# One-hot rows of the expert picks on VectorE, and a three-subtraction split on GpSimd, in an attention and mixture-of-experts kernel

## The chip, the cores and the metric

The kernel runs on one core of a Trainium2 chip. The metric is the device time of one execution in microseconds (us). The engines are named as in the profile: PE is TensorE, DVE is VectorE, ACT is ScalarE, POOL is GpSimd, and SP (SPq its queue) issues most transfers. TENSOR_TENSOR is an elementwise operation with two tensor inputs, TENSOR_SCALAR one with a tensor and constants, CAST a copy that changes the type.

## The reference

Input x is 8 sequences of 512 rows of 128 numbers. The first layer is a linear attention with Fourier features, 16 heads of 8:

```python
q = x @ Wq.T + bq; k = x @ Wk.T + bk; v = x @ Wv.T + bv          # split into 16 heads of 8
feat(z) = concat(cos(z @ proj / sqrt(8)), sin(z @ proj / sqrt(8))) / sqrt(128)
kv  = sum over the rows l of feat(k)[l] (outer) v[l]              # per sequence and head
x   = layernorm(x + (feat(q) @ kv) @ Wo.T + bo)
```

The second layer routes each row to 2 of 8 experts (128 to 512 to 128, with relu):

```python
route = softmax(x @ Wr + br); keep the two largest, divide by their sum
x = layernorm(x + sum over the 2 picks of route[e] * (relu(x @ W1[e] + b1[e]) @ W2[e] + b2[e]))
```

Everything is float32 in and out.

## The kernel before

The program is written out by hand: each engine has its own list of instructions, in order, and semaphores tie the lists together. No planner is at work; the number u at which a piece stands in an engine's loop is the order.

**Attention stage.** Eight bodies, one for each sequence b, 16 units u each. Units 0 to 7 are keys, units 8 to 15 queries; a unit is 128 x 1024 angles. For each unit PE multiplies into the PSUM tensor `ang` (L570, L574), DVE rounds to whole turns (`round_turns`, L1067), PE subtracts the turns (L583), ACT takes two sines (L873, L874), and the second is squared (`square`), on POOL for u in (1, 3, 4, 6, 8, 10, 12) (L1430) and on DVE for the others (L1075). PE then uses the features in `kv_product` (L603, keys) and `out_product` (L638, queries). In body b the loops of DVE and POOL square unit u - 2 at step u.

**Pieces of other sequences in body b.** ACT evacuates k and q of sequence b + 1 (L859 a bf16 part, L861 the float32 value `qk_f`), and POOL splits each into three bf16 parts (`split`, L354, L356, L358, at u = 7 and u = 9), which SP writes to DRAM and reads back stacked. For sequence b - 1 comes the end of the first layer and the routing: `residual`, `statistics`, `moments` (DVE), `rsqrt` (POOL), `normalize` (ACT), logits (PE, L665), `take_logits` and `largest` (DVE, u = 10), `which` (DVE, u = 10, after the square of that step: the indices of the picks, `idx8`, as u32). At u = 11 POOL runs `chosen`: it makes two one-hot rows of 8 from each row's picks (`hot`), adds them (`picks`, L1542), and writes three numbers beside the row that will be sent. PE counts ranks from `picks` (`ranks`, L675 to L680, at u = 12), DVE adds the base (`slot_m`, L1141, u = 12), POOL multiplies by `hot` (L1553, u = 13), DVE reduces to slot numbers, and POOL sends the rows to their expert's region with eight indirect transfers (L1561, u = 14 and 15). PE's list at u = 12 is: the angles, L583 of the unit before, `kv_turn` (L614 to L617), `ranks`; then u = 13 with L574, L583 and `out_product` (L638), which waits for the DVE evacuation `kv_evac` (L1086, L1087), which stands behind `round_turns` of unit 12. DVE's list at u = 11 is `round_turns`, `kvT_evac` (L1079), `square` of unit 9.

In body 7 there is no split. POOL builds the table of expert tiles for the first six sequences in its place (`early_counts` to `early_table`, L1454 to L1502), and `chosen(6)` stands behind it.

**Expert stage.** 71 tiles of 128 rows. SP loads a tile, PE turns it and runs the two layers (L775, L786, L795), DVE evacuates (L1306, L1314, L1354), ACT copies the weights and scales, POOL adds a bias for some tiles (L1572) and sends the results (L1591). The routing of sequence 7 is interleaved: `which` at DVE's tile step 18, `chosen` at POOL's step 20, `ranks` at PE's step 22. Last, the two picks of each row are summed and normalized.

A `hold` in the code is a wait. `over` broadcasts a tensor; `idx8` is 128 x 4 x 8 u32, `iota` the numbers 0 to 7.

Of the kernel before, what the change touches and what calls it, by code (L numbers as in the profile page):

```python
# [23 lines left out]
ALU = mybir.AluOpType  # L24
# [67 lines left out]
def build(nc, x, proj, Wq, bq, Wk, bk, Wv, bv, Wo, bo, W1, b1, W2, b2, Wr, br,  # L92
# [8 lines left out]
    with ctx:  # L101
        def sb(name, shape, dt=F32):
            return ctx.enter_context(nc.sbuf_tensor(name, shape, dt))
# [38 lines left out]
        lg = sb("lg", [P, LT, EXP])  # L142
        top8 = sb("top8", [P, LT, EXP])
        idx8 = sb("idx8", [P, LT, EXP], U32)
        pick_no = sb("pick_no", [P, LT, TOPK])
        hot = sb("hot", [P, TOPK, LT, EXP])
        picks = sb("picks", [P, LT * EXP], F16)
        slot_m = sb("slot_m", [P, LT, EXP])
# [60 lines left out]
        def cut(n):  # L209
# [38 lines left out]

            "y_ok", "bo_ok", "ln_stat", "ln_aggr", "ln_eps", "ln_pow", "ln_shift", "xn_ok", "xr_mm", "xr_ev",

            "lg_mm", "lg_ok", "top_ok", "idx_ok", "no_ok", "off_ok", "hot_ok", "picked", "meta", "rk_mm", "slot_ok", "based",
            "slotk_ok", "slots_ok", "scattered", "pads_at", "pads_in", "rt", "tab_ok",

            "et", "et_half", "w1_in", "w2_in", "b1_in", "b2_in", "b1_mm", "b1_ok", "bp_mm", "bp_ev", "b2_mm", "b2_ok", "gap_ok", "gate_ok", "xbg_ok",
# [64 lines left out]
        def over(v, shape):  # L319

            return v.broadcast_to(shape)
# [21 lines left out]
        def sequences(body):  # L343

            for b in range(BATCH):
                body(b, b % RING)

        def split(eng, b, side):

            wait(eng, "kq"[side] + "_ev", 1, b, 1)  # L350
            f = qk_f[:, side, :]
            p = parts[:, side, :, :]
            n = 3 * side
            eng.tensor_tensor(f, f, p[:, 0, :], ALU.subtract).then_inc(s["split"], 1)  # L354
            hold(eng, "split", 6, b, n + 1)
            eng.tensor_copy(p[:, 1, :], f).then_inc(s["split"], 1)  # L356
            wait(eng, "split", 6, b, n + 2)
            eng.tensor_tensor(p[:, 2, :], f, p[:, 1, :], ALU.subtract).then_inc(s["split"], 1)  # L358
# [634 lines left out]
        def _(dve):  # L993
# [135 lines left out]
            def which(b):  # L1129
# [2 lines left out]
                    ins = dve.max_index(idx8[:, t, :], top8[:, t, :], lg[:, t, :])  # L1132
                ins.then_inc(s["idx_ok"], 1)

            n_picks = LT * EXP

            def take_ranks(b):
# [109 lines left out]
            LAST_ROUND = ((7, bias_add), (8, bias_add))  # L1247

            BEFORE_ROUND = ((6, moments), (10, take_logits), (13, move_base))
            AFTER_ROUND = ((5, residual), (10, largest))  # L1250
            AFTER_SQUARE = ((5, statistics), (10, which), (12, take_ranks), (13, slot_numbers))

            def body(b, ph):
                first = isinstance(b, int) and b == 0
                last = isinstance(b, int) and b == BATCH - 1
                for u in range(UNITS):
# [33 lines left out]
                    if u == 15 and not last:  # L1290
# [4 lines left out]
            square(e, -2)  # L1295
            square(e, -1)

            LAST_PIECES = ((1, residual), (2, statistics), (3, moments), (16, take_logits), (17, largest), (18, which),
                           (23, take_ranks), (24, move_base), (26, slot_numbers))
            LATE_TABLE = ((27, late_counts), (29, late_ends), (31, late_starts), (32, late_table))  # L1300

# [119 lines left out]
        def _(pool):  # L1421
# [84 lines left out]
            def body(b, ph):  # L1506
                first = isinstance(b, int) and b == 0
                last = isinstance(b, int) and b == BATCH - 1
                for u in range(UNITS):
                    if not (first and u < 2):  # L1510
                        square(b, u - 2)
                    if u == 6 and not first:
                        rsqrt(1, b - 1, 0)
                    for step, piece in (EARLY_TABLE if last else ()):
                        if u == step:
                            piece()
                    if u in (7, 9) and not last:
                        split(pool, b + 1, (u - 7) // 2)
                    if first and u >= 11:
                        add_bo(pool, u - 9)  # L1520
                    if b == 1 and u == 0:
                        add_bo(pool, BATCH - 1)
                    if u == 11 and not first:
                        chosen(b - 1)
                    if u == 13 and not first:
                        slots_of_picks(b - 1)
                    if u in (14, 15) and not first:
                        send_rows(b - 1, u - 14)

            def chosen(b):  # L1530

                hold(pool, "idx_ok", 1, b, 1)
                pool.tensor_copy(pick_no[:, :, :], idx8[:, :, 0:TOPK]).then_inc(s["no_ok"], 1)
                wait(pool, "no_ok", 1, b, 1)
                for k in range(TOPK):
                    ins = pool.tensor_tensor(hot[:, k, :, :], over(iota[:, :].unsqueeze(1), tile8),
                                             over(pick_no[:, :, k:k + 1], tile8), ALU.subtract)
                ins.then_inc(s["off_ok"], 1)
                hold(pool, "off_ok", 1, b, 1)
                pool.tensor_scalar(hot[:, :, :, :], hot[:, :, :, :], 0.0, None, ALU.is_equal).then_inc(s["hot_ok"], 1)  # L1540
                wait(pool, "hot_ok", 1, b, 1)
                pool.tensor_tensor(picks[:, :], hot[:, 0, :, :].rearrange("p t e -> p (t e)"),  # L1542
                                   hot[:, 1, :, :].rearrange("p t e -> p (t e)"), ALU.add).then_inc(s["picked"], 1)
                pool.tensor_tensor(rows_s[:, :, P + 2:XW], top8[:, :, 0:1], top8[:, :, 1:2], ALU.subtract)
                pool.tensor_copy(rows_s[:, :, P:P + 1], pick_no[:, :, 0:1])
                pool.tensor_scalar(rows_s[:, :, P + 1:P + 2], rows_s[:, :, P + 1:P + 2], float(LEN), None, ALU.add)\
                    .then_inc(s["meta"], 1)

            def slots_of_picks(b):

# [98 lines left out]
```

## Time and profile before

| | |
|---|---|
| median of 3 runs | 553.1 us (549.98 to 554.34) |
| profiled execution, its own time | 551.36 us |
| its span in the trace | 549.6 us |
| granted clock of TensorE, mean | 0.959 of full |
| PE busy | 483.9 us, 88% |
| DVE busy | 427.8 us, 78% |
| POOL busy | 410.7 us, 75% |
| ACT busy | 381.0 us, 69% |

Busy times are shares of the whole span, over stages with different limits. Busy time of POOL and DVE contains time in which an instruction has begun and stands still. The attention stage fills the span up to about 360 us, the expert stage follows to about 522 us, and the sums and the last normalization close it.

### The profile page before, as it was taken

The numbers are of one execution on the slowest core, as the hardware profiler recorded it, in microseconds if no ns is written. First come the engines' busy times: TensorE is split into PE (matmuls) and PEld (weight loads), VectorE is DVE, ScalarE is ACT, GpSimd is POOL, SyncE is SP. The second block draws the span as 40 slices with busy tenths as digits, with TensorE's granted clock in tenths as the row PEclk, the third lists the DMA queues.
The fourth block names the chain that finished last, engine by engine and source line by source line (L and its number), as shares of the span: only waits on it lengthen the run. The fifth ranks groups of instructions, "written<-read, shape, count | busy, mean of one in ns | idle before, by whom it ended". The sixth has DMA issues, their size and how long they took to land.

```text
span 549.6 us, 13153 instructions
## 1 busy us (share of the span) xinstructions
PE 483.9 (88%) x4205; PEld 297.4 (54%) x4205; DVE 427.8 (78%) x907; ACT 381.0 (69%) x533; POOL 410.7 (75%) x474
## 2 busy tenths in 40 slices
PE   6698889999999999999999989689999679999914
PEld 3333344444444444444344444158999678999802
DVE  6769978988988988988988888568677475777654
ACT  2686669789789789789789689376555244565325
POOL 2279549879879889879879889857677656777645
PEclk9899989999999999999999999799999789999957
DMA  4675504705704705604605400032222123222174
GB/s 96 169 228 160 127 1 138 195 16 144 203 20 126 206 17 144 190 16 141 153 15 136 126 17 1 8 84 58 69 65 71 59 75 94 70 65 70 39 273 191
DMA packets 44447, 56.03 MB, mean 102 GB/s; under 512 B 8779, under 2 KB 31541, under 8 KB 44381
## 3 DMA queue, kind: packets, MB, share of 16 engines
q1 hardware_dynamic: 39493, 45.86, 30.5%
q0 software_dynamic: 4320, 8.95, 5.0%
q8 instruction: 36, 0.59, 0.5%
q10 hardware_dynamic: 568, 0.38, 0.2%
q14 instruction: 30, 0.25, 0.2%
HBM read 37.22 MB, written 17.94 MB: 100 GB/s over the span
## 4 chain that ended last, share of the span: by engine, by line
PE 55%; POOL 12%; DVE 12%; issue 9%; ACT 6%; DMA 2%; another core or an unknown queue 2%; SPq 1%; DVEq 0%; ACTq 0%; POOLq 0%
PE ang L786 11%; PE ang L795 10%; PE misc L603 7%; PE ang L583 5%; PE misc L638 5%; DVE turns L1067 5%; DVE feats L1075 4%; POOL feats L1430 3%; PE ang L574 3%; PE ang L570 3%; POOL routed_dram L1561 2%; PE misc L512 2%; PE misc L649 2%; ACT rows_s L893 2%
## 5 line engine op out<-in xcount | busy, mean ns | idle before, releaser
L1067 DVE TENSOR_SCALAR turns<-ang 128x1024 f16<-128x1024 f32 x128 | 155.4, 1217 | 46.4 <-PE ang L574 23.4
L873 ACT ACTIVATE feats<-ang 128x1024 f32<-128x1024 f32 x128 | 131.7, 1029 | 63.6 <-PE ang L583 61.1
L1430 POOL TENSOR_TENSOR feats<-feats 128x1024 f32<-128x1024 f32 x56 | 107.0, 1910 | 48.8 <-ACT feats L874 48.4
L874 ACT ACTIVATE feats<-ang 128x1024 f32<-128x1024 f32 x128 | 131.5, 1028 | 0.0
L1075 DVE TENSOR_TENSOR feats<-feats 128x1024 f32<-128x1024 f32 x72 | 102.5, 1423 | 0.7 <-ACT feats L874 0.6
L1591 POOL DMA_INDIRECT expert_dram<-feats x71 | 69.7, 981 | 36.3 <-DVE feats L1354 28.5
L1561 POOL DMA_INDIRECT routed_dram<-rows_s,slots x64 | 76.3, 1193 | 20.7 <-issue 18.3
L583 PE MATMUL ang<-turns,negi 128*128 128x512 f16 x256 | 77.9, 386 | 12.4 <-DVE turns L1067 10.5
L795 PE MATMUL ang<-experts,feats 128*128 x568 | 77.6, 281 | 5.5 <-DVE feats L1314 5.4
L786 PE MATMUL ang<-feats 128*128 128x128 f32 x568 | 78.1, 282 | 4.5 <-DVE feats L1306 2.2
L944 ACT ACTIVATE feats<-experts 128x644 f32 x71 | 52.5, 739 | 36.8 <-DVE feats L1354 25.3
L786 PEld LDWEIGHTS ang<-feats 128*128 128x128 f32 x568 | 70.6, 195 | 8.4 <-issue 5.2
L795 PEld LDWEIGHTS ang<-experts,feats 128*128 128x128 f32 x568 | 70.8, 196 | 6.8 <-issue 6.8
L603 PE MATMUL misc<-feats,v_pad 128*32 128x256 f32 x1024 | 70.7, 396 | 0.0
L1314 DVE TENSOR_TENSOR feats<-ang,feats 128x512 f32<-128x512 f32 x71 | 49.0, 690 | 26.5 <-PE ang L786 13.8
L638 PE MATMUL misc<-feats,kv_pad 128*32 128x512 f32 x512 | 67.8, 617 | 0.6
L570 PEld LDWEIGHTS ang<-proj_stk,stk 72*128 72x128 bf16 x512 | 30.9, 98 | 34.4 <-issue 32.6
L603 PEld LDWEIGHTS misc<-feats,v_pad 128*32 128x32 f32 x1024 | 27.3, 111 | 40.3 <-issue 29.2
L961 ACT ACTIVATE feats<-feats 128x128 f32<-128x128 f32 x71 | 28.1, 395 | 27.6 <-DVE feats L1363 20.4
L570 PE MATMUL ang<-proj_stk,stk 72*128 72x128 bf16 x512 | 39.9, 221 | 2.0 <-ACT stk L912 1.4
L583 PEld LDWEIGHTS ang<-turns,negi 128*128 128x128 f16 x256 | 21.7, 99 | 32.9 <-DVE turns L1067 15.6
L574 PE MATMUL ang<-stk,proj_stk 72*128 72x512 bf16 x128 | 39.1, 388 | 0.0
(195 smaller groups left out, 597.2 us busy)
## 6 DMA issues: line engine op xcount, KB each, us to landing
stk<-parts_dram SPq DMA_DIRECT2D x189, 96.0 KB
parts_dram<-parts SPq DMA_DIRECT2D x16, 384.0 KB, 3.6
feats<-routed_dram SPq DMA_DIRECT2D x72, 65.5 KB
feats<-expert_dram SPq DMA_DIRECT2D x16, 256.0 KB, 5.4
x_all<-attn_x SPq DMA_DIRECT2D x8, 256.0 KB, 4.8
experts<-ffn_W SPq DMA_DIRECT2D x8, 256.0 KB
out<-feats SPq DMA_DIRECT2D x8, 256.0 KB, 2.2
x_in<-attn_x SPq DMA_DIRECT2D x7, 256.0 KB
```

The costliest lines, as they stand in the source:

```text
L570: mm = pe.matmul(a[:, at:at + FEAT], stk[:, 0, hg, g, tok:tok + P], proj_stk[:, :], start=(g == 0), stop=False, skip_group_check=True)
L583: mm = pe.matmul(ang[:, slot(ph, u), t * 512:(t + 1) * 512], negi[:, :], turns[:, u % 2, t * 512:(t + 1) * 512], start=False, stop=True, s ...
L603: mm = pe.matmul(misc[32 * g:32 * g + 32, 0, 0:2 * FEAT].rearrange("p (a m) -> p a m", a=2), v_pad[:, 2 * half + t, g, hg * PADH:(hg + 1) ...
L638: mm = pe.matmul(misc[32 * g:32 * g + 32, 1, :], kv_pad[:, a, g, hg * PADH:(hg + 1) * PADH], feats[:, 2 * hg + g // 2, a, (g % 2) * LEN:(g ...
L786: mm = pe.matmul(h_bank[r % 2][:, j * P:(j + 1) * P], w_now[:, r % W_RING, j * P:(j + 1) * P], xgT[:, r % 2, :], start=True, stop=True)
L795: mm = pe.matmul(y_bank[r % 2][:, 0:P], hidT[:, r % 2, j * P:(j + 1) * P], expert(x_e)[:, j * P:(j + 1) * P], start=(j == 0), stop=(j == H ...
L873: act.activation(f[:, 0, :], a, ACT.Sin, scale=TWO_PI)
L874: act.activation(f[:, 1, :], a, ACT.Sin, scale=TWO_PI / 2).then_inc(s["sines"], 1)
L1067: dve.tensor_scalar(turns[:, u % 2, :], ang[:, slot(ph, u), :], MAGIC, -MAGIC, ALU.add, ALU.add)\
L1075: dve.tensor_tensor(f, f, f, ALU.mult).then_inc(s["sq_v"], 1)
L1430: pool.tensor_tensor(f, f, f, ALU.mult).then_inc(s["sq_p"], 1)
L1561: pool.indirect_dma_start(routed_dram, bass.IndirectOffsetOnAxis(slots[:, k, t:t + 1], 0), rows_s[:, t, :], None).then_inc(s["scattered"], 16)
```

## The change

DVE gets a piece `one_hot` that compares `iota` with the u32 indices directly, in two TENSOR_TENSORs, at u = 11 between `kvT_evac` and the square (in the expert stage at tile step 19). POOL's `chosen` loses the CAST of the indices, the two subtractions and the comparison with zero; it writes the three numbers beside the row first, waits for `hot_ok`, and then adds the one-hot rows. The split of k and q on POOL becomes three subtractions: the second part is written by a subtraction with bf16 output, the remainder by the same subtraction in float32, the third part as before. DVE's own split of sequence 0 stays.

```diff
-        pick_no = sb("pick_no", [P, LT, TOPK])
+        def split_apart(eng, b, side):
+            wait(eng, "kq"[side] + "_ev", 1, b, 1)
+            f = qk_f[:, side, :]
+            p = parts[:, side, :, :]
+            n = 3 * side
+            eng.tensor_tensor(p[:, 1, :], f, p[:, 0, :], ALU.subtract).then_inc(s["split"], 1)
+            wait(eng, "split", 6, b, n + 1)
+            eng.tensor_tensor(f, f, p[:, 0, :], ALU.subtract).then_inc(s["split"], 1)
+            wait(eng, "split", 6, b, n + 2)
+            eng.tensor_tensor(p[:, 2, :], f, p[:, 1, :], ALU.subtract).then_inc(s["split"], 1)
...
+            def one_hot(b):
+                hold(dve, "idx_ok", 1, b, 1)
+                for k in range(TOPK):
+                    ins = dve.tensor_tensor(hot[:, k, :, :], over(iota[:, :].unsqueeze(1), tile8),
+                                            over(idx8[:, :, k:k + 1], tile8), ALU.is_equal)
+                ins.then_inc(s["hot_ok"], 1)
...
-            AFTER_ROUND = ((5, residual), (10, largest))
+            AFTER_ROUND = ((5, residual), (10, largest), (11, one_hot))
...
-            LAST_PIECES = (... (18, which),
+            LAST_PIECES = (... (18, which), (19, one_hot),
...
                     if u in (7, 9) and not last:
-                        split(pool, b + 1, (u - 7) // 2)
+                        split_apart(pool, b + 1, (u - 7) // 2)
...
             def chosen(b):
                 hold(pool, "idx_ok", 1, b, 1)
-                pool.tensor_copy(pick_no[:, :, :], idx8[:, :, 0:TOPK]).then_inc(s["no_ok"], 1)
-                wait(pool, "no_ok", 1, b, 1)
-                for k in range(TOPK):
-                    ins = pool.tensor_tensor(hot[:, k, :, :], over(iota[:, :].unsqueeze(1), tile8),
-                                             over(pick_no[:, :, k:k + 1], tile8), ALU.subtract)
-                ins.then_inc(s["off_ok"], 1)
-                hold(pool, "off_ok", 1, b, 1)
-                pool.tensor_scalar(hot[:, :, :, :], hot[:, :, :, :], 0.0, None, ALU.is_equal).then_inc(s["hot_ok"], 1)
+                pool.tensor_tensor(rows_s[:, :, P + 2:XW], top8[:, :, 0:1], top8[:, :, 1:2], ALU.subtract)
+                pool.tensor_copy(rows_s[:, :, P:P + 1], idx8[:, :, 0:1])
+                pool.tensor_scalar(rows_s[:, :, P + 1:P + 2], rows_s[:, :, P + 1:P + 2], float(LEN), None, ALU.add)\
+                    .then_inc(s["meta"], 1)
                 wait(pool, "hot_ok", 1, b, 1)
                 pool.tensor_tensor(picks[:, :], ...
```

The last three instructions of `chosen` before are the same three that now stand at its head, with `pick_no` in the place of `idx8`.

## Rows read from the trace of the kernel before

**Rows 1.** Busy time by stretch: stretch, length, busy of each engine, PE clock, DMA share, GB/s
```profile
172.00:213.00 41.00, 39.30 (x363) 18.38 (x362) 35.77 (x57) 35.58 (x42) 35.80 (x36) 1.00 0.41 116
```

**Rows 2.** Chain of waits, body 4, 185 to 232 us: start, us, what
```profile
218.36 0.14 PE misc L675
...
219.12 0.43 PE ang L583 x2
...
219.66 1.92 PE misc L638 x16
```

**Rows 3.** Timeline of POOL, body 4: start, us, line, operation [idle before]
```profile
204.33 1.16 POOL L354 TENSOR_TENSOR qk_f<-qk_f,parts 128x512 f32<-128x512 f32 x1
205.56 1.48 POOL L356 CAST parts<-qk_f 128x512 bf16<-128x512 f32 x1
207.12 1.15 POOL L358 TENSOR_TENSOR parts<-qk_f,parts 128x512 bf16<-128x512 f32 x1
...
210.09 1.16 POOL L354 TENSOR_TENSOR qk_f<-qk_f,parts 128x512 f32<-128x512 f32 x1
211.31 1.49 POOL L356 CAST parts<-qk_f 128x512 bf16<-128x512 f32 x1
...
215.84 0.19 POOL L1533 CAST pick_no<-idx 128x8 f32<-128x8 uint32 x1
...
216.64 1.29 POOL L1540 TENSOR_SCALAR hot<-hot 128x64 f32<-128x64 f32 x1
218.01 0.25 POOL L1542 TENSOR_TENSOR picks<-hot 128x32 f16<-128x32 f32 x1
```

**Rows 4.** Timeline of DVE, body 4
```profile
204.39 2.18 DVE L1075 TENSOR_TENSOR feats<-feats 128x1024 f32<-128x1024 f32 x1
...
210.95 1.38 DVE L1075 TENSOR_TENSOR feats<-feats 128x1024 f32<-128x1024 f32 x1
...
216.46 1.22 DVE L1075 TENSOR_TENSOR feats<-feats 128x1024 f32<-128x1024 f32 x1
217.59 1.22 DVE L1067 TENSOR_SCALAR turns<-ang 128x1024 f16<-128x1024 f32 x1
...
219.02 0.41 DVE L1087 COPY kv_pad<-misc 128x256 f32<-128x256 f32 x1
```

**Rows 5.** One line's instructions on POOL: count, shortest/median/longest ns, first and last start
```profile
L356 POOL CAST parts<-qk_f x14: 609/1484/1491, 35.9 to 294.4; 128x512 bf16<-128x512 f32 x14
```

**Rows 6.** Timeline of POOL, body 0
```profile
40.39 2.14 POOL L354 TENSOR_TENSOR qk_f<-qk_f,parts 128x512 f32<-128x512 f32 x1
42.59 0.61 POOL L356 CAST parts<-qk_f 128x512 bf16<-128x512 f32 x1
```

**Rows 7.** Timeline of DVE, body 0
```profile
39.78 1.73 DVE L1075 TENSOR_TENSOR feats<-feats 128x1024 f32<-128x1024 f32 x1
```

**Rows 8.** Groups of DVE by line: count, busy us, mean ns, idle before
```profile
L1141 DVE TENSOR_TENSOR slot_m<-misc,base 128x32 f32<-128x32 f32 x8 | 1.5, 182 | 3.2 <-PE misc L680 3.2
```

**Rows 9.** Timeline of POOL, body 7
```profile
324.08 1.89 POOL L1430 TENSOR_TENSOR feats<-feats 128x1024 f32<-128x1024 f32 x1 [1.62 <-ACT feats L874]
...
346.35 0.19 POOL L1533 CAST pick_no<-idx 128x8 f32<-128x8 uint32 x1
...
347.15 0.38 POOL L1540 TENSOR_SCALAR hot<-hot 128x64 f32<-128x64 f32 x1
347.62 0.25 POOL L1542 TENSOR_TENSOR picks<-hot 128x32 f16<-128x32 f32 x1
```

**Rows 10.** Timeline of PE, body 7
```profile
347.93 0.21 PE L675 MATMUL misc<-picks,tri 128*128 128x32 f16 x1 [4.52 <-POOL picks L1542]
```

**Rows 11.** Busy time by stretch, body 7 behind that wait
```profile
349.00:353.00 4.00, 4.00 (x19) 0.71 (x17) 2.71 (x5) 1.94 (x2) 3.60 (x4) 0.50 0.00 0
```

**Rows 12.** Timeline of DVE, expert stage: the COPY of tile step 19
```profile
408.29 0.28 DVE L1306 COPY feats<-ang 128x128 f32<-128x128 f32 x1
```

**Rows 13.** Timeline of POOL, expert stage: the first transfer behind `chosen(7)`
```profile
408.62 1.09 POOL L1591 DMA_INDIRECT expert_dram<-feats  x1 [0.16 <-issue]
```

More of the change, by code:

```diff
@@ L249, in build @@
             "y_ok", "bo_ok", "ln_stat", "ln_aggr", "ln_eps", "ln_pow", "ln_shift", "xn_ok", "xr_mm", "xr_ev",
-            "lg_mm", "lg_ok", "top_ok", "idx_ok", "no_ok", "off_ok", "hot_ok", "picked", "meta", "rk_mm", "slot_ok", "based",
+            "lg_mm", "lg_ok", "top_ok", "idx_ok", "hot_ok", "picked", "meta", "rk_mm", "slot_ok", "based",
             "slotk_ok", "slots_ok", "scattered", "pads_at", "pads_in", "rt", "tab_ok",
@@ L1296, in _ @@
             square(e, -1)
-            LAST_PIECES = ((1, residual), (2, statistics), (3, moments), (16, take_logits), (17, largest), (18, which),
+            LAST_PIECES = ((1, residual), (2, statistics), (3, moments), (16, take_logits), (17, largest), (18, which), (19, one_hot),
                            (23, take_ranks), (24, move_base), (26, slot_numbers))
@@ L1543, in chosen @@
                                    hot[:, 1, :, :].rearrange("p t e -> p (t e)"), ALU.add).then_inc(s["picked"], 1)
[L1544 to L1547, printed above, removed]
             def slots_of_picks(b):
```

## The prediction, before the changed kernel was run

> **What bounds the kernel now.** I read the busy time by stretch first, to see whether an engine is full where the change acts. In one body of the attention stage PE works 39.30 of 41.00 us at full clock, DVE, ACT and POOL about 35.7 each [rows 1]. The chain of waits inside such a body then says who sets the end: around unit 12 it runs from one PE instruction into the next, the rank count at 218.36, the turns at 219.12, the query product at 219.66, with DVE just keeping up [rows 2]. Bodies 1 to 6 repeat this pattern; body 4 stands for the six. The timelines of POOL and DVE, laid side by side, show how close the other engines are. The sum of the one-hot rows, `picks`, is done at 218.26, a tenth before PE wants it [rows 3, 2]. `kv_pad` is done at 219.43, and PE starts on it at 219.66, a tenth after it was free at 219.55 (219.12 + 0.43) [rows 4, 2]. `round_turns` of unit 12 is done at 218.81, and PE uses it at 219.12 [rows 4, 2]. So POOL and DVE have almost no slack exactly at unit 12.
>
> Only in body 7 does a long wait stand: PE idles 4.52 us for `picks`, until 347.93 [rows 10], behind POOL's tile table. POOL itself had idled 1.62 us for ACT at 324.08 [rows 9], so what makes POOL faster ahead of 324 us can't shorten that wait beyond what ACT allows.
>
> **POOL and DVE block one another.** This decides the costs. A DVE square takes 1.22 us when nothing is in its way (216.46) [rows 4]. The one at 204.39 took 2.18 and ended at 206.57; POOL's subtraction beside it ended at 205.49, 1.08 earlier [rows 4, 3]. The one at 210.95 ended at 212.33; the subtraction beside it at 211.25, again 1.08 earlier [rows 4, 3]. The CASTs behind these subtractions end at 207.04 and 212.80, each 0.47 behind the square [rows 3, 4]. A CAST takes 0.61 when free [rows 6] and 1.48 here, and the median of 14 is 1.484 with the longest 1.491 [rows 5]: a constant, since POOL holds off the square and the square then holds off the CAST. A POOL subtraction behind a square does the same: 2.14 at 40.39, end 42.53, the square beside it ended at 41.51 (39.78 + 1.73), 1.02 earlier [rows 6, 7]. The Trainium skill has this as a rule ("SBUF — State Buffer", Who interferes with whom): GpSimd and a VectorE instruction with two SBUF inputs want the same port pair, which is locked for a whole instruction, and the one that comes second stands still. The trace agrees, in these three ends. By that rule `one_hot`, with two SBUF inputs, joins the contenders, which speaks against this change.
>
> **The split.** By the durations as they stand, three subtractions at 1.16 in the place of 1.16 + 1.48 + 1.15 save 0.32 us [rows 3], 0.64 for the two of a body. I don't take this. Free, the middle step goes from 0.61 to 1.16 [rows 6, 3], and it will meet the same square, so it costs 0.55 more: the subtraction ends at the square's end + 1.02, where the CAST ended at + 0.47. The first split ends 0.55 later. The work behind it moves with it, the second first subtraction ends at 211.80, the square of 210.95 at 212.88, and the second split ends 1.10 late. What hides it: POOL's lateness is no one's wait until step 11, and SP has most of a body to move the parts. If that cover is gone, it is 1.1 us a body. The Trainium skill puts GpSimd's two-input operations at a floor of about 2.5 cycles an element and calls one-input ones roughly line-rate ("GPSIMD Engine Reference", Elementwise — side-by-side cycle accounting, and Engine selection). By it a subtraction costs more than the CAST that it replaces, though the page of the profile shows 1.48 against 1.16; the free CAST of 0.61 agrees.
>
> **`chosen`, bodies 1 to 6.** Gone: everything from 215.84 to 218.01, 2.17 us [rows 3]. Of the comparison's 1.29 us only 0.38 is its own (347.15, DVE idle) [rows 9]; the rest is the square of 216.46, and whoever stands there next inherits it. So 1.27 is really gone, and POOL is 1.10 late by the split. Both about cancel. POOL's square ahead of `chosen` now ends near 217.0 instead of 215.9.
>
> **`one_hot` on DVE.** The nearest row is `slot_m`, of the same shape, 182 ns [rows 8]; two in a pipeline cost some 0.2 us if free. They would start at 216.46, where the square starts now [rows 4], and POOL's late square holds the port until 217.0. So they pass at 217.0 to 217.2, and DVE's square starts at 217.2 instead of 216.46. Behind it stand `round_turns` of unit 12, `slot_m` and `kv_evac`, all 0.7 late; PE has 0.1 of slack, so it takes 0.6 to 0.7. POOL's four short operations (about 0.2 each) stand partly behind that square, so `picks` is done at 218.65 to 219.1 instead of 218.26, and the ranks are 0.4 to 0.8 late on PE. These overlap and are not added. Bounds: 0.2 us a body if nothing blocks, 1.1 if POOL's short operations get the port ahead of `one_hot` and DVE's square starts at 217.6. I take 0.7, for it follows from the ends above; nothing later in the body gives it back, as the rest waits for PE. Six bodies: +4.2 (1.2 to 6.6).
>
> **Body 7.** No split here. From the start of `chosen(6)`, 346.35, to the end of `picks`, 347.87, are 1.52 us [rows 9]. New: four short operations at about 0.2, some 0.75; `hot` is long there. The wait of 4.52 [rows 10] shrinks by 0.8, and PE is late next by what is left, 3.7. PE's clock then still falls to its lower level, 0.50 [rows 11]; were it not to, the 4 us of that stretch would be 2.0 shorter. -0.8 (to -2.8).
>
> **The rest.** Body 0 has two splits and no `chosen`; squares there move both ways by about half a microsecond. I take 0, keep 0.5 each way. In the expert stage `one_hot` stands at DVE's step 19, ahead of the COPY at 408.29 [rows 12]; POOL, waiting for it, would send its next transfer at about 408.9 instead of 408.62 [rows 13], 0.3 later, and PE reads `picks` two tiles on. 0, at most 0.3.
>
> **Sum.** +4.2 - 0.8 = +3.4 us, against the profiled execution's 551.36: 554.8. Its span is 549.6, with 1.8 around it. The median of the three runs, 553.1, is 1.7 higher; all four average 552.2. From that, 555.6; I say 555.5.
>
> **Rivals.**
> *The change is hidden.* The port counts for little: `one_hot` costs its 0.2 six times, body 7 gives 0.8: +0.4, 552.5. For it: POOL is on no wait of PE in bodies 1 to 6. Against it: the constant ends.
> *A gain.* As above, and the clock holds in body 7: +1.2 - 2.8 = -1.6, about 550.5. For: it needs only a shorter wait. Against: 3.7 us of idling remain. A gain of over 1% (5.5 us) would need the whole wait gone, for which POOL would have to leave ACT behind at 324 us.
> *Slower than a measurement can hide.* At 215.84 the first of POOL's short operations starts with no pause behind the square. If POOL so keeps the port, its three ready ones (0.6) pass first, `one_hot` gets through at 217.6 to 217.8, and DVE's square at 217.8 is 1.3 late; PE then loses 1.3 a body: +7.8 - 0.8 = +7.0, 559.2. It decides from 1.05 us a body on. The Trainium skill says issue order decides who blocks ("SBUF — State Buffer", Who interferes with whom); no row here shows the order for this pair.
> *It doesn't do what it says.* The split drops a CAST but adds a subtraction: on POOL it saves nothing. That is part of the forecast.
>
> **Chances.** Over 1% is what a measurement of this kernel can tell from no change. Forecast 0.58, of it 0.12 with over 1.05 us a body net; hidden 0.20; gain 0.10, of it 0.04 over 1%; the slower rival 0.12. So faster 0.04, same 0.72, slower 0.24. Range: from the gain with its offset, 550, to the slower rival, 559.5. The forecast's own is 552 to 559.
>
> **What would show it.** Right: the middle step of the split at about 2.0 us in 13 of 14, not 1.16; the square of unit 9 starting 0.7 later after step 11 and lasting about 1.2, or starting on time and lasting longer; PE waiting for DVE ahead of L638 or for `picks` at L675 in bodies 1 to 6; these bodies 41.7 us long instead of 41.0; the wait for `picks` in body 7 at 3.7. Wrong: a middle step at 1.16 with the square at 1.22 beside it; bodies of 41.0; or a POOL that the split makes so late that PE waits for one of its squares.

## The result: 5.7% slower, where 0.6% was forecast

The changed kernel takes 583.62 us (median of 4 runs, 579.69 to 587.75), the kernel before 552.23 beside it (549.98 to 554.34). The ratio is 1.057, interval [1.048, 1.066]. I had forecast 555.5 and a range of 550 to 559.5. The profiled execution took 584.74 us, its span is 582.9 where it was 549.6, and the mean granted clock fell from 0.959 to 0.930.

The parts that I had costed came out near their forecast. First POOL in body 3 of the changed kernel (start, us, operation, idle before): the split and the sum of the one-hot rows.

```profile
177.13 1.16 POOL L353 TENSOR_TENSOR parts<-qk_f,parts 128x512 bf16<-128x512 f32 x1
178.37 2.03 POOL L355 TENSOR_TENSOR qk_f<-qk_f,parts 128x512 f32<-128x512 f32 x1
180.48 1.16 POOL L357 TENSOR_TENSOR parts<-qk_f,parts 128x512 bf16<-128x512 f32 x1
...
190.05 1.20 POOL L1554 TENSOR_SCALAR rows_s<-rows_s 128x4 f32<-128x4 f32 x1
191.23 0.24 POOL L1557 TENSOR_TENSOR picks<-hot 128x32 f16<-128x32 f32 x1
```

The middle step takes 2.03 us where the CAST took 1.48 [rows 3, 5]; the square beside it (177.19, 2.18 us, below) ends at 179.37, the step 1.03 later. DVE in the same body:

```profile
177.19 2.18 DVE L1086 TENSOR_TENSOR feats<-feats 128x1024 f32<-128x1024 f32 x1
...
189.27 0.72 DVE L1150 TENSOR_TENSOR hot<-iota,idx 128x32 f32<-128x32 f32 x2
189.91 1.24 DVE L1086 TENSOR_TENSOR feats<-feats 128x1024 f32<-128x1024 f32 x1
```

The two comparisons take 0.72, some 0.5 more than the 0.2 I took as free, and push the square behind them; in [rows 4] nothing stands ahead of that square. PE then waits 0.36 us for `picks` ahead of the ranks, and in body 7 still 3.98 where it was 4.52 [rows 10] (3.7 was forecast):

```profile
191.53 0.19 PE L686 MATMUL misc<-picks,tri 128*128 128x32 f16 x1 [0.36 <-POOL picks L1557]
...
385.19 0.21 PE L686 MATMUL misc<-picks,tri 128*128 128x32 f16 x1 [3.98 <-POOL picks L1557]
```

What I had not looked for is in the waits of the whole kernel (engine, tile and line, what it waited for: us in total, times, longest):

```profile
DVE turns L1078 <- remote: 21.1, 5, 4.8
PE ang L594 <- DVE turns L1078: 20.1, 13, 3.9
ACT feats L884 <- remote: 18.1, 4, 4.6
```

The view writes "remote", and the chain "another core", where it finds no releaser; this program has one core. The chain of the body has it as one piece:

```profile
154.74 1.21 DVE feats L1086
155.95 4.74 another core or an unknown queue
160.70 0.02 issue
160.72 1.23 DVE turns L1078
162.00 1.04 PE ang L594 x2
```

Beside it stand PE's and DVE's timelines:

```profile
154.09 0.62 PE L581 MATMUL ang<-proj_stk,stk 72*128 72x128 bf16 x8
...
157.84 0.23 PE L581 MATMUL ang<-proj_stk,stk 72*128 72x128 bf16 x1 [0.43 <-issue]
162.00 1.04 PE L594 MATMUL ang<-turns,negi 128*128 128x512 f16 x2 [3.92 <-DVE turns L1078]
```

```profile
154.74 1.21 DVE L1086 TENSOR_TENSOR feats<-feats 128x1024 f32<-128x1024 f32 x1
160.72 1.22 DVE L1078 TENSOR_SCALAR turns<-ang 128x1024 f16<-128x1024 f32 x1 [4.77 <-remote]
```

`round_turns` at 160.72 needs the angles that PE is recorded as making from 154.09 to 154.71, and DVE was free at 155.95. ACT and SyncE go on at 160.76 and 160.81 too. Everything that waits for PE stands still at once and goes on at once. Such a stall stands at the head of each of the bodies 2 to 7, 3.4 to 5.1 us long (by what DVE waits); none stands in body 1, for POOL sends nothing at the end of body 0. The one of body 7 looks different: there PE's own matmuls (L707, L581) are recorded in small groups from 342.63 to 348.55, with 0.2 to 1.0 us of idle time between them, and DVE waits 5.07 us for them by name. What it does to a body is read by stretch (stretch, length, busy time of PE, PEld, DVE, ACT, POOL, clock, DMA share, GB/s), against [rows 1]:

```profile
149.00:197.00 48.00, 41.78 (x366) 18.85 (x362) 36.83 (x59) 35.66 (x44) 34.18 (x32) 0.93 0.38 104
```

A body lasts 48.00 us, not 41.00. PE is busy 2.48 longer for the same matmuls, at a clock of 0.93 where it was 1.00, and idle 4.52 longer (6.22 against 1.70). The clock falls only once the stall has begun and PE has stood still from 158.07 on; 0.50 is the lower of its two levels, 1.2 GHz:

```profile
157.00:159.00 2.00, 0.64 (x8) 0.33 (x6) 0.00 (x0) 0.00 (x0) 1.60 (x2) 1.00 0.47 136
159.00:161.00 2.00, 0.00 (x0) 0.00 (x0) 0.28 (x1) 0.24 (x1) 0.31 (x1) 0.61 0.12 40
161.00:163.00 2.00, 1.00 (x6) 0.17 (x8) 2.00 (x3) 1.70 (x2) 0.00 (x0) 0.50 0.43 130
```

The sum closes. From POOL's first send at the end of body 1 to that at the end of body 6 are 236.79 us (101.12 to 337.91), before 206.33 (100.79 to 307.12): +30.46, or 4.6 to 6.9 a body, the change's own part included. From there to the first send of body 7 are 53.50 (to 391.41) against 47.02 (to 354.14): +6.48. Ahead of all that lies +0.33. The rest is 3.97 shorter: the chain before had pieces of 4.19 and 3.19 us of the same unnamed kind there (428.19 and 438.47), the one after has a single one of 3.50. Together +33.3, the whole difference of the spans.

### The profile page after: what moved, and what is told of

It is laid out like the page before. It is cut to its first block, busy times and chain, and to the rows that moved or that the text cites. A ratio compares the mean times of both kernels' runs of the same rounds, so it can differ in the third digit from the quotient of the medians.

```text
span 582.9 us, 13137 instructions
## 1 busy us (share of the span) xinstructions
PE 497.4 (85%) x4205; PEld 300.2 (51%) x4205; DVE 431.7 (74%) x923; ACT 381.0 (65%) x533; POOL 396.8 (68%) x442
## 4 chain that ended last, share of the span: by engine, by line
PE 54%; DVE 16%; issue 10%; ACT 6%; POOL 6%; another core or an unknown queue 3%; DMA 2%; SPq 1%; DVEq 0%; POOLq 0%; ACTq 0%
PE ang L797 11%; PE ang L806 10%; PE misc L649 9%; DVE turns L1078 8%; PE ang L594 6%; PE ang L581 5%; PE misc L614 4%; DVE feats L1086 4%; PE ang L585 2%; PE misc L523 2%; ACT rows_s L904 2%; POOL feats L1449 2%; PE misc L529 1%; PE misc L660 1%
## 5 line engine op out<-in xcount | busy, mean ns | idle before, releaser
L1078 DVE TENSOR_SCALAR turns<-ang 128x1024 f16<-128x1024 f32 x128 | 155.4, 1216 | 80.4 <-PE ang L581 33.3
L1449 POOL TENSOR_TENSOR feats<-feats 128x1024 f32<-128x1024 f32 x56 | 113.3, 2024 | 100.8 <-ACT feats L885 100.6
L594 PE MATMUL ang<-turns,negi 128*128 128x512 f16 x256 | 82.5, 405 | 28.2 <-DVE turns L1078 20.1
L1572 POOL DMA_INDIRECT routed_dram<-rows_s,slots x64 | 64.6, 1009 | 19.9 <-issue 18.3
L649 PE MATMUL misc<-feats,kv_pad 128*32 128x512 f32 x512 | 73.4, 662 | 1.1 <-DVE base L1165 1.1
L581 PEld LDWEIGHTS ang<-proj_stk,stk 72*128 72x128 bf16 x512 | 32.8, 102 | 43.6 <-issue 40.1
L581 PE MATMUL ang<-proj_stk,stk 72*128 72x128 bf16 x512 | 43.1, 230 | 4.8 <-issue 2.9
```

The costliest lines, as they stand in the source:

```text
L581: mm = pe.matmul(a[:, at:at + FEAT], stk[:, 0, hg, g, tok:tok + P], proj_stk[:, :], start=(g == 0), stop=False, skip_group_check=True)
L594: mm = pe.matmul(ang[:, slot(ph, u), t * 512:(t + 1) * 512], negi[:, :], turns[:, u % 2, t * 512:(t + 1) * 512], start=False, stop=True, s ...
L649: mm = pe.matmul(misc[32 * g:32 * g + 32, 1, :], kv_pad[:, a, g, hg * PADH:(hg + 1) * PADH], feats[:, 2 * hg + g // 2, a, (g % 2) * LEN:(g ...
L1078: dve.tensor_scalar(turns[:, u % 2, :], ang[:, slot(ph, u), :], MAGIC, -MAGIC, ALU.add, ALU.add)\
L1449: pool.tensor_tensor(f, f, f, ALU.mult).then_inc(s["sq_p"], 1)
```

## What stands beside the stall: POOL's sends

One other thing had changed at that place. POOL sends eight pieces of the routed rows there, from its step 14 on. Before, at the end of body 3, with DVE beside it:

```profile
183.01 1.12 POOL L1561 DMA_INDIRECT routed_dram<-rows_s,slots  x1 [0.17 <-issue]
184.44 1.98 POOL L1561 DMA_INDIRECT routed_dram<-rows_s,slots  x1 [0.30 <-issue]
186.72 0.96 POOL L1561 DMA_INDIRECT routed_dram<-rows_s,slots  x1 [0.30 <-issue]
187.98 1.54 POOL L1561 DMA_INDIRECT routed_dram<-rows_s,slots  x1 [0.30 <-issue]
```

```profile
184.36 1.22 DVE L1075 TENSOR_TENSOR feats<-feats 128x1024 f32<-128x1024 f32 x1
```

And after, at the end of body 2:

```profile
149.25 1.11 POOL L1572 DMA_INDIRECT routed_dram<-rows_s,slots  x1 [0.17 <-issue]
150.66 0.96 POOL L1572 DMA_INDIRECT routed_dram<-rows_s,slots  x1 [0.30 <-issue]
151.93 1.06 POOL L1572 DMA_INDIRECT routed_dram<-rows_s,slots  x1 [0.30 <-issue]
153.29 0.96 POOL L1572 DMA_INDIRECT routed_dram<-rows_s,slots  x1 [0.30 <-issue]
...
158.35 0.95 POOL L1572 DMA_INDIRECT routed_dram<-rows_s,slots  x1 [0.31 <-issue]
```

```profile
150.94 1.22 DVE L1086 TENSOR_TENSOR feats<-feats 128x1024 f32<-128x1024 f32 x1
```

Before, a DVE square starts 1.35 us behind the first send (184.36 against 183.01), just ahead of the second at +1.43, and the second takes 1.98 instead of 0.96. After, the square comes at +1.69, just behind the second at +1.41, and holds nothing up. The change moved it by 0.3 us. The eight then run 0.3 us apart, in 10.05 us instead of 11.8. Not all of that is the cause of the stall: it begins at +6.7, before the seventh send (+7.84), and the later sends are quick also because DVE stands still and no square of it meets them. Theory 1 was that the dense run brings the stall. The rivals were the one-hot rows or the late split by themselves, and SyncE's transfers in that stretch.

## The experiments

They were run in five sets, each on one chip beside the kernel before, which took 550.3, 536.6, 552.4, 537.6 and 548.5 us in them. The chips have the numbers 8, 0, 9, 9 and 11 in the record: number 9 is there once with 552.4 and once with 537.6. So ratios are compared, and by kind of set: in the two of 537 us no trace of a variant has a stall, which makes them blind for the stall and clean for the rest.

**First set: each half alone, and the sends spaced.** `e1_split_only` is the kernel before with the new split:

```diff
                     if u in (7, 9) and not last:
-                        split(pool, b + 1, (u - 7) // 2)
+                        split_apart(pool, b + 1, (u - 7) // 2)
```

> Only the split is changed (three subtractions on GpSimd); the one-hot rows stay on GpSimd as before. Theory 1, the eight sends of routed rows: the stall of 4.8 us at the head of each body comes when POOL's eight indirect transfers run unhindered beside SP's loads; in the kernel before, a VectorE square holds off two of them by 1.0 and 0.6 us. By it the time jumps by 20 to 35 us if the sends here run at 0.96 each, and stays within 6 us of before if they are held off as before. Theory 2, the port contest alone: the split is 1.1 us late per body, all hidden: within 2 us of before. Theory 3, the late split pushes SP's loads into the sends: slower by 20 us or more here, whatever the pace of the sends.

Measured: 554.14 us, ratio 1.0087 [1.0045, 1.0129], no stall in the attention stage, the second send held up as before. But the bodies are 42.2 us long (first sends at 99.84, 142.26, 184.48, 226.84). The late split isn't hidden: the chain runs through POOL from 202.38 to 221.08, and PE waits, where before it didn't:

```profile
221.12 0.19 PE L687 MATMUL misc<-picks,tri 128*128 128x32 f16 x1 [1.16 <-POOL picks L1554]
```

`e2_picks_only` is the changed kernel with the old split:

```diff
                     if u in (7, 9) and not last:
-                        split_apart(pool, b + 1, (u - 7) // 2)
+                        split(pool, b + 1, (u - 7) // 2)
```

> Only the one-hot rows are changed (VectorE, two comparisons); the split is that of before. Theory 1 (sends unhindered): DVE's order at units 12 to 15 is later by 0.2 to 0.7 us against POOL's, so the sends may start ahead of the square and run at 0.96: then 20 to 35 us slower, with stalls that end on PE's angles. Theory 2 (port contest alone): 0.2 to 0.7 us a body, 1 to 4 us slower. Theory 3 (late split): no more than 4 us slower.

Measured: 582.37 us, ratio 1.0568 [1.0499, 1.0636]. All of the loss comes with the one-hot rows on DVE; the square stands at +1.68 and the sends are dense.

`e3_paced_sends` leaves the change whole and spaces the sends:

```diff
                 for t in tiles:
+                    if (k, t) in idle:      # ((0, 2), (1, 0)): ahead of the third and the fifth
+                        pool.tensor_tensor(idle_t[:, LT * k + t, :], eps_t[:, :], half_t[:, :], ALU.pow)
                     pool.indirect_dma_start(routed_dram, ...
```

> The changed kernel, with two idle operations of about 1.04 us (a power of 128 x 4 numbers that nothing reads) on POOL, ahead of the third and the fifth of the eight sends in bodies 1 to 7, so that the burst takes about 12.3 us instead of 10.1, as long as in the kernel before. Theory 1: the stalls of 4.8 us shrink to under 1 us and the time falls from 583 to 553 to 560. Theories 2 and 3: no gain, 583 to 586.

Measured: 550.41 us, ratio 0.9995 [0.9955, 1.0036]: two useless instructions more in every body, and 32 us less than `e2_picks_only` in the same set. The square is still at +1.68 and the first two sends are as quick as after, but the run is broken (timeline of POOL, spaced sends):

```profile
182.50 1.10 POOL L1575 DMA_INDIRECT routed_dram<-rows_s,slots  x1 [0.17 <-issue]
183.90 0.97 POOL L1575 DMA_INDIRECT routed_dram<-rows_s,slots  x1 [0.30 <-issue]
184.89 1.41 POOL L1574 TENSOR_TENSOR idle_t<-eps_t,half_t 128x4 f32<-128x4 f32 x1
186.50 1.03 POOL L1575 DMA_INDIRECT routed_dram<-rows_s,slots  x1 [0.20 <-issue]
```

Bodies are 41.67 us. So without the stall the change costs 0.67 a body, one-hot rows and split together (0.7 was forecast). That the ratio is 1.000 all the same fits the expert stage: the trace of the kernel before loses 7.4 us to unnamed pieces there, this one none.

`e4_weights_early` moves SyncE's loads of the experts' weights ahead of its stacked reads:

```diff
                 load_x(b + 1)
-                stack(b)
                 if b <= 3:
                     load_second(3 * (b - 1), min(3 * b, EXP))
...
+                stack(b)
```

> The changed kernel, with SP's loads of expert weights moved ahead of the stacked reads of the same body (they are issued behind the load of x, in the part of a body in which no DMA runs), so that the sends meet only the tail of the stacked reads. If theory 1 needs a full DMA beside the sends, the stall goes or shrinks to 2 us or less and the time falls to 553 to 565. If the sends alone do it, or the port contest, it stays at 580 to 586.

Measured: 584.85 us, ratio 1.0625 [1.0557, 1.0692], stalls of 2.0 to 5.3 us. The weight loads aren't needed for the stall.

**Second set, of 537 us.** Four kernels; the edits of three of them stand with their repetition in the third set:

> The kernel before (550.3 us in the first set) with nothing of the change, only five idle adds of VectorE (about 0.07 us each, 0.35 together) ahead of its square of unit 15, so that this square starts behind GpSimd's second indirect send (at about +1.7 us from the first send) and no longer ahead of it (+1.35). Theory 1 (sends that nothing holds up bring the stall of about 4.8 us): the sends last 0.95 to 1.1 us each, the stall comes in bodies 2 to 7, 575 to 590 us. Rival (the stall belongs to the one-hot rows on VectorE or to the order of GpSimd's work around the picks): no stall, six or seven times 0.35 us at most, 550 to 553 us.

> The kernel after with three idle adds of GpSimd (some 0.45 us together) ahead of the first indirect send, so that VectorE's square comes at about +1.2 us from it and holds the second send up again, as in the kernel before. Theory 1: the second send lasts about 2 us, the stalls go, bodies of about 42 to 43 us, 550 to 558 us in spite of the added work. Rival (what counts is the change's own work): the stalls stay, 583 to 588 us.

> The kernel after, where SyncE's reads of the stacked keys and values of side 1, and the weight loads behind them, wait until the indirect sends of the body have landed. If the stall needs the sends and SyncE's transfers together: no stall, 548 to 560 us, unless the later reads make TensorE wait. If the sends alone do it: the stall of about 4.8 us stays in bodies 2 to 7, 580 to 590 us, and the reads come later beside.

Measured, with the kernel before at 536.6: 1.0027 [0.9999, 1.0055], 1.0075 [1.0049, 1.0102] and 1.0063 [1.0035, 1.0090]. The phases were as planned, but no kernel stalled, e9 not either, whose first four sends are as dense as the changed kernel's. Its DVE has the next square at +4.80 from the first send, where the changed kernel has it at +5.49 (154.74): there the word from PE is late before the long stall begins. In e6 the squares keep meeting the later sends (the fifth takes 1.29 us, the sixth 1.96). By the first ratio theory 1 would have fallen, had this set been able to show the stall. The changed kernel wasn't in it, and that was the gap in my plan. The fourth, `e8_sends_split`, sends four pieces at unit 14 and four at unit 4 of the next body:

```diff
-                    if u in (14, 15) and not first:
-                        send_rows(b - 1, u - 14)
+                    if u == 14 and not first:
+                        send_rows(b - 1, 0)      # body 7 sends all eight
+                    if u == 4 and isinstance(b, int) and b >= 2:
+                        send_rows(b - 2, 1)
```

> The kernel after with its eight indirect sends of a body in two groups of four, the second group at unit 4 of the next body (the last body sends all eight). Theory 1 in the form that a run of eight unhindered sends is what fills something up: no stall, or one of under 1 us, bodies of 41.5 to 43 us, 548 to 558 us. Rival (any unhindered sends do it, however few): stalls of half the length in two places, 575 to 585 us. The four sends at unit 4 stand ahead of other work of GpSimd; if its squares become late there, up to 1 us a body more.

Measured: 1.0403 [1.0339, 1.0468], without a stall: bodies of 44.2 us, for the second four make POOL's square and the `rsqrt` behind it late, and through ACT that reaches PE, which waits 2.7 us for `qk_f`. A repetition in another 537 us set gave 1.0369 [1.0327, 1.0411]. On the stall it says nothing.

The repetition's text:

> The changed kernel with its sends in two groups of four, 13 us apart, a second time, on a chip where the kernel before takes about 551 us if this is one. In the second set it took 1.040 of the kernel before with no stall, 44.2 us a body, for the second group makes GpSimd's squares late. If four unhindered sends are too few for a stall: again 1.04. If they are enough: stalls besides, ratio 1.06 or more.

**Third set: the same with the changed kernel as a control.** Here the kernel before took 552.4 us.

> The changed kernel itself, unaltered, beside the kernel before in one set. In the second set the kernel before took 536.6 us (550.3 in the first) and no kernel of it showed the stall, so it has to be told apart whether the stall is there on this chip. If the stall goes with the kernel alone: ratio 1.05 to 1.06, stalls of 3.4 to 5 us in bodies 2 to 7, whatever the kernel before takes. If the stall goes with the chip or the set as well: where the kernel before takes about 537 us, the changed one takes 539 to 542 us (0.65 us a body and little else, ratio 1.005 to 1.01), no stall; where it takes about 550 us, ratio 1.055.

Measured: 587.48 us, ratio 1.0642 [1.0586, 1.0698], stalls in bodies 2 to 7. So this set can show them. The next kernel is the decisive one. It is the kernel before with nothing of the change:

```diff
 # VectorE, in the kernel before
+                    if u == 15 and not first:
+                        for n in range(5):
+                            dve.tensor_tensor(idle_v[:, n, :], zero_t[:, :], eps_t[:, :], ALU.add)
                     if not (first and u < 2):
                         square(b, u - 2)
```

> The kernel before with five idle adds of VectorE ahead of its square of unit 15, a second time, beside the changed kernel. If f1 stalls and theory 1 is right (a run of sends that nothing holds up at its head is enough): stalls as in f1, ratio 1.04 to 1.06. If f1 stalls and this one doesn't: the phase of the square alone isn't the cause, ratio 1.00 to 1.01. If f1 doesn't stall: ratio 1.003 as in the second set.

Measured: 582.61 us, ratio 1.0568 [1.0504, 1.0632]. Its DVE in the first body with sends, which begin at 100.14:

```profile
101.47 0.46 DVE L1275 TENSOR_TENSOR idle_v<-zero_t,eps_t 128x4 f32<-128x4 f32 x5
101.86 1.21 DVE L1076 TENSOR_TENSOR feats<-feats 128x1024 f32<-128x1024 f32 x1
...
105.65 1.22 DVE L1076 TENSOR_TENSOR feats<-feats 128x1024 f32<-128x1024 f32 x1
110.99 1.23 DVE L1068 TENSOR_SCALAR turns<-ang 128x1024 f16<-128x1024 f32 x1 [4.12 <-remote]
```

Five idle adds, some 0.4 us together, put the square at +1.72, and cost 30 us. They are some 3 us of work in all, and in the 537 us set they cost 0.3%. This shows without anything of the change that the place of DVE's work against the sends is enough to bring the loss; by which step, it doesn't show.

The third kernel is the reverse, the changed kernel with its sends 0.5 us later:

```diff
+                    if u == 14 and not first:
+                        for n in range(3):
+                            pool.tensor_tensor(idle_p[:, n, :], zero_t[:, :], eps_t[:, :], ALU.add)
                     if u in (14, 15) and not first:
                         send_rows(b - 1, u - 14)
```

> The changed kernel with three idle adds of GpSimd ahead of the first send, a second time, beside the changed kernel. If f1 stalls: by theory 1 no stall, ratio 1.007 to 1.015; by the rival the stalls stay, ratio 1.055. If f1 doesn't stall: ratio 1.007 as in the second set.

Measured: 560.88 us, ratio 1.0161 [1.0101, 1.0221]. The square is at +1.23 and the second send takes 1.86 again. The early bodies are nearly free of stalls (42.7, 42.4, 42.4 us, with one wait of 0.88 us in the first). Later ACT waits 2.50 us once (to 241.35), two unnamed pieces of 2.64 and 1.96 us stand in body 7, and two of 3.40 come later. So holding the second send takes most of the stall away, not all.

The fourth, `f4_quiet_queue_again`, is the changed kernel with SyncE's reads of one side held back until the sends have landed:

```diff
                     write(side)
+                    if side == 1 and b > 1:
+                        sp.wait_ge(s["scattered"], 16 * TOPK * LT * (b - 1))
                     for hg in range(HG):
```

> The changed kernel with SyncE's stacked reads of side 1 and its weight loads held back until the body's sends have landed, a second time, beside the changed kernel. If f1 stalls: no stall here would mean that sends and SyncE's transfers are needed together (ratio 1.005 to 1.015), stalls of some 4.8 us that the sends alone do it (ratio 1.05). If f1 doesn't stall: ratio 1.006 as in the second set.

Measured: 579.97 us, ratio 1.0494 [1.0419, 1.0569]. The first two stalls are smaller, the later ones stay. By stretch, around the one at 196.24 to 199.67 (the sends begin at 189.55):

```profile
189.00:191.00 2.00, 2.00 (x20) 0.47 (x12) 1.21 (x3) 1.85 (x3) 1.52 (x3) 1.00 0.00 0
191.00:193.00 2.00, 2.00 (x25) 1.53 (x18) 1.84 (x3) 1.46 (x2) 1.70 (x2) 1.00 0.21 67
193.00:195.00 2.00, 2.00 (x19) 0.61 (x16) 1.41 (x2) 1.07 (x2) 1.39 (x3) 1.00 0.13 34
195.00:197.00 2.00, 1.83 (x14) 0.78 (x14) 1.24 (x2) 0.87 (x1) 1.70 (x2) 1.00 0.23 73
197.00:199.00 2.00, 0.76 (x12) 0.45 (x8) 0.00 (x0) 0.00 (x0) 1.39 (x3) 1.00 0.20 57
```

SyncE issues nothing from 183 to 201.00 us, the DMA share is 0.23 at most, and the stall comes all the same. SyncE's transfers aren't needed for it, nor full DMA engines. They may lengthen it, for the two smaller stalls are unexplained.

**Fourth set (537 us) and fifth: how much of a pause.**

> The kernel before with the two idle power operations of GpSimd (about 1.04 us each) ahead of the third and the fifth indirect send, nothing of the change. If a run of sends too dense costs the kernel before something too (it has stalls of 4.2 and 3.2 us in the expert stage and bodies up to 41.9 us instead of 41.0): 545 to 549 us where the kernel before takes 551, ratio 0.988 to 0.998. If the pacing only adds work: ratio 1.000 to 1.005. The changed kernel with the same pacing had ratio 0.9995, so by the port contest of 0.65 us in six bodies this one should be 4 us below it, ratio 0.992.

Measured, with the kernel before at 537.6: 564.54 us, 1.0504 [1.0463, 1.0545], a clear miss, and not by a stall (there is none). In the kernel before the square holds the second send already; two more instructions bring five of the eight to 1.7 to 2.0 us (POOL is busy 40.34 of the 45 us from 145 us on, against 35.80 of 41 in [rows 1]), and the chain of waits runs through POOL, at bodies of 45.4 to 46.7 us. The same two instructions are harmless in the changed kernel, whose first sends are quick. The same 2 us of idle work on POOL is worth -32 us in the one and +27 in the other.

> The one-hot rows on VectorE with the old split, and the paced sends of g1. If only the stall and the port contests count: between g1 and the changed kernel with paced sends (0.9995). By my forecast the whole 0.65 us a body is the one-hot rows' (ratio 1.000); by what the split alone cost (1.1 us a body longer) part of it is the split's (ratio 0.993 to 0.997).

Measured: 1.0035 [1.0011, 1.0058], bodies of 41.25 us; with the new split and one pause, in the same set, bodies of 41.57. So of the change's own price the one-hot rows are some 0.25 us a body, against the 41.0 of [rows 1] (41.05 in e6, in a set of 537 us), and the split some 0.3.

The one pause is this, in the changed kernel:

```diff
-                        send_rows(b - 1, u - 14)
+                        send_rows(b - 1, u - 14, idle=((1, 0),))
```

> The changed kernel with one idle power operation of GpSimd, ahead of the fifth send only: two runs of four sends with about 1.1 us between them. If a run of eight unhindered sends is needed: no stall, ratio 1.00 to 1.01 (on a chip where the kernel before takes about 551 us). If four are enough, or the start of the run counts (the kernel before holds up its second and fourth): stalls of 2 to 5 us, ratio 1.03 to 1.055.

Measured: 1.0030 [1.0008, 1.0051], where nothing stalls. The last set repeated it with the changed kernel beside it, the kernel before at 548.5:

> The changed kernel, unaltered. Where the kernel before takes about 537 us: by the variants measured there (one pause in the sends 1.003, reads held back 1.006, sends later 1.0075) ratio 1.003 to 1.008, bodies of 41.6 us and no stall; if the changed kernel stalls wherever it runs, ratio 1.05. Where the kernel before takes about 551 us: ratio 1.057 to 1.064 as twice before.

> The changed kernel with one idle power operation of GpSimd ahead of the fifth send. Where the kernel before takes about 537 us: 1.003 again. Where it takes about 551 us: if a run of more than four unhindered sends is needed, ratio 1.00 to 1.01 and no stall; if four are enough, stalls and 1.03 to 1.055.

Measured: the changed kernel 587.26, ratio 1.0686 [1.0618, 1.0754]; with one pause 552.67, ratio 1.0081 [1.0038, 1.0124]. POOL of the latter:

```profile
143.08 0.96 POOL L1575 DMA_INDIRECT routed_dram<-rows_s,slots  x1 [0.30 <-issue]
144.06 1.06 POOL L1574 TENSOR_TENSOR idle_t<-eps_t,half_t 128x4 f32<-128x4 f32 x1
145.31 1.33 POOL L1575 DMA_INDIRECT routed_dram<-rows_s,slots  x1 [0.19 <-issue]
```

One instruction of 1.06 us a body between the fourth and the fifth send is worth 34.6 us. With four dense sends, a pause of 1.27 us and four more, no long stall comes; without the pause it does. But the loss isn't wholly gone. Bodies are 42.3 us here and were 41.6 with the same kernel where nothing stalls, and ACT twice waits unnamed for 2.9 us, the first time from 99.57 on, 2.9 us behind the first send of its body. The 0.7 us stand in DVE's timeline, here first, from a body whose sends begin at 139.04, then in g2, where they begin at 141.00:

```profile
143.38 1.23 DVE L1079 TENSOR_SCALAR turns<-ang 128x1024 f16<-128x1024 f32 x1 [0.58 <-PE ang L582]
```

```profile
144.67 1.21 DVE L1079 TENSOR_SCALAR turns<-ang 128x1024 f16<-128x1024 f32 x1
```

The angles come at +4.34 instead of +3.67, before the pause has begun. In `e3_paced_sends`, with a pause ahead of the third send too, the same instruction starts at +3.67 (144.50 from 140.83) in a set where `e2_picks_only` stalls. So PE's word is late already after three dense sends, and the pause keeps it from growing. No version beat the kernel before.

## Why the prediction was wrong

**The step that failed** is the end of "`one_hot` on DVE": "I take 0.7 ... nothing later in the body gives it back, as the rest waits for PE". It took a later square of DVE to be a later square and no more. I carried the port's rule through the split, the comparison and the one-hot rows, and stopped there. POOL's eight sends stood in the timeline of the same body, one of them at 1.98 us where its neighbours take 0.96, with a DVE square 0.08 us ahead of it (184.36 against 184.44). That row asked what happens if the square comes 0.1 us later. It should have been a rival of its own. I could not have known its price, and f2 shows +30 us in the whole kernel for a shift of this kind; by the stretches the worst bodies of the changed kernel are 6.9 us longer, with the clock that the stall takes along and the change's own 0.7. Why PE's word comes late once the sends are dense stays open.

**"What hides it: POOL's lateness is no one's wait until step 11"** was false by itself. With the old `chosen`, the split's 1.10 us come out as 1.16 us of PE's waiting and 42.2 us a body (e1). In the whole change the shorter `chosen` pays for most of that, as the forecast had it ("Both about cancel"): some 0.3 us a body are left (g2 against g3).

**The sum without the stall came out right, partly by luck.** 0.7 a body was forecast for the one-hot rows alone, with the split at nothing, and 0.67 measured for the whole change (e3). But that is shared between rows (about 0.25) and split (about 0.3 to 0.4): one term was too large and the other missing, and the two errors cancel. The middle step of the split at 2.0 us was right (mean 1.96 of 14). Body 7 was to wait 3.7 for `picks` and waited 3.98, and the clock fell there as forecast.

**The chances.** Slower by over 1% had 0.24, with the longest rival at 559.2. All three rivals that give a time priced the same mechanism, the port at unit 12, with other sizes, one of them with the clock in body 7 besides. None asked about the other transfers and instructions that a shift of 0.3 us would move past each other.

## What to carry to other kernels

When a change shifts one engine by some tenths of a microsecond, list every pair of instructions on two engines that start within that distance of one another, and ask of each what happens if their order turns. A row that takes twice as long as its like (1.98 against 0.96) marks such a pair, and it may be doing a service: here it spaced a run of indirect sends. Where such sends stand in a row, put useful work between them rather than let chance do it, ahead of the third already, and run the changed kernel itself in every set of experiments, for a set may not show the effect at all.

## What the runs showed of the hardware

- When GpSimd makes indirect sends with 0.3 us between them, a stretch of 3.4 to 5.1 us follows in which all engines that wait for PE stand still, though PE's matmuls are mostly recorded as done. It begins some 6.7 us behind the first send (149.25 to 155.95), so before all eight are out, and single waits begin at +2.9 (99.57 against 96.67 in `h2_one_gap_again`). One pause of about 1.3 us behind the fourth prevents the long part (ratio 1.069 to 1.008). How many dense sends it takes isn't shown. Nor does a run show why the word from PE comes late: PE's records may be early, or PE itself may be slowed, as its broken groups in body 7 suggest. Every execution has a span and a granted clock on record, so presumably each ran with the profiler on; whether the stall comes without it isn't shown either.
- It depends on the set: in two of five the kernel before took 537 us instead of 549 to 552, and none of the variants stalled there. In the others the kernel before loses to something like it as well (4.19 and 3.19 us in its expert stage). What differs isn't known; as chip number 9 stands for a set of either kind, the number of the chip alone doesn't decide it. The changed kernel was never in a set of 537 us, so whether it would stall there wasn't seen.
- An indirect send of GpSimd is held up by a two-input DVE square that starts first (1.98 against 0.96 us). The square isn't (1.22). The Trainium skill ("SBUF — State Buffer", Who interferes with whom) says that a DMA stalled by a VectorE instruction is one whose descriptors GpSimd writes, and the trace agrees, in that what is held up is GpSimd's own sending instruction; it also reports a probe in which `tensor_tensor` didn't stall a DMA, and infers why. Here a `tensor_tensor` does hold a send up, and the measurement decides. Whether it is the writing of descriptors that waits or the reading of the slots from SBUF, no run shows.
